# All steady projections, values and outputs in two turns on the array's 64-row halves, a job's first turn ahead of the sums

## The reference

```python
attn_in  = adaln(x, cond, ln1...)
x = attn(attn_in, attn_in, sa_wq, sa_wkv, sa_wo, sa_bo) + x      # 16 heads of 64
cross_in = adaln(x, cond, ln1...)
x = attn(cross_in, layernorm(context), ca_wq, ca_wkv, ca_wo, ca_bo) + x
x = gelu(adaln(x, cond, ln2...) @ ff_w1 + ff_b1) @ ff_w2 + ff_b2 + x
```

## Time and profile before

| | us |
|---|---|
| median of three runs | 1116.58 (1114.38 to 1116.66) |
| the profiled execution, its own time | 1118.88 |
| its span in the trace | 1117.1 |
| TensorE busy | 1097.2 (98%) |
| VectorE busy | 858.1 (77%) |
| GpSimd busy | 775.7 (69%) |
| ScalarE busy | 636.9 (57%) |

### The profile page before, as it was taken

How to read it: one execution, slowest core, us unless ns; L and a number is a source line. 1 busy time by engine, 2 the same in 40 slices (tenths; PEclk the granted TensorE clock), 3 DMA queues, 4 the chain that set the end, 5 groups by cost and what they waited for, 6 DMA issues and landing times.

```text
span 1117.1 us, 18312 instructions
## 1 busy us (share of the span) xinstructions
PE 1097.2 (98%) x6904; PEld 785.1 (70%) x6904; DVE 858.1 (77%) x1023; ACT 636.9 (57%) x895; POOL 775.7 (69%) x503
## 2 busy tenths in 40 slices
PE   8989999999999999999999999999999999989998
PEld 7657666776666776666766667766666776756997
DVE  5878887878787777878888777777877777788554
ACT  6465565665666555577665555555555545775521
POOL 2687887787788767789799766777777667755210
PEclk9899999999999999999999999999999999999999
DMA  6312121311231111211121112211121111300001
GB/s 175 86 46 57 32 53 39 89 30 30 53 77 38 39 36 23 72 39 39 29 63 38 39 39 59 51 23 36 38 72 39 37 31 30 114 1 1 20 19 38
DMA packets 59606, 52.31 MB, mean 47 GB/s; under 512 B 23040, under 2 KB 42496, under 8 KB 59264
## 3 DMA queue, kind: packets, MB, share of 16 engines
q1 hardware_dynamic: 57632, 49.57, 18.5%
q10 hardware_dynamic: 1888, 1.59, 0.5%
HBM read 15.22 MB, written 2.10 MB: 16 GB/s over the span
## 4 chain that ended last, share of the span: by engine, by line
PE 90%; DVE 5%; ACT 2%; issue 1%; DMA 1%; SPq 0%; POOL 0%; ACTq 0%; POOLq 0%; DVEq 0%
PE ps L872 18%; PE ps L713 12%; PE ps L715 11%; PE ps L714 11%; PE ps L813 6%; PE ps L860 6%; PE ps L848 5%; PE ps L819 5%; PE ps L815 5%; PE ps L817 5%; PE ps L963 4%; DVE lo L1083 1%; PE ps L729 1%; DMA x<-x_dram 1%; DVE w_lo L1117 1%
## 5 line engine op out<-in xcount | busy, mean ns | idle before, releaser
L548 ACT ACTIVATE probs<-ps 128x1024 f32<-128x1024 f32 x256 | 262.5, 1027 | 208.0 <-PE ps L819 183.6
L1065 DVE TENSOR_REDUCE neg_max<-ps 128x2 f32<-128x1024 f32 x256 | 301.6, 1226 | 76.7 <-PE ps L848 76.7
L420 POOL TENSOR_TENSOR acc<-acc,probs 128x1024 f32<-128x1024 f32 x128 | 306.2, 2392 | 18.6 <-POOL acc L415 0.4
L872 PE MATMUL ps<-probs,v 128*64 128x512 f32 x1024 | 230.7, 592 | 0.0
L415 POOL TENSOR_TENSOR acc<-probs 128x1024 f32<-128x1024 f32 x64 | 153.2, 2394 | 72.1 <-ACT probs L548 72.1
L872 PEld LDWEIGHTS ps<-probs,v 128*64 128x64 f32 x1024 | 73.9, 137 | 146.1 <-issue 146.1
L429 POOL TENSOR_TENSOR eo<-tmp 128x512 f32<-128x512 f32 x63 | 89.7, 1424 | 120.2 <-DVE tmp L1092 120.1
L1092 DVE TENSOR_TENSOR tmp<-ps,rope 128x1024 f32<-128x1024 f32 x126 | 148.2, 1211 | 4.5 <-PE ps L715 4.3
L813 PE MATMUL ps<-max_rows,pick 64*128 64x512 f32 x512 | 109.3, 419 | 2.6 <-DVE o_lo L1079 1.6
L713 PE MATMUL ps<-xn_hi,w_hi 128*128 128x512 f32 x256 | 107.8, 421 | 2.5 <-DVE o_lo L1079 1.3
L848 PE MATMUL ps<-hi 64*128 64x512 f32 x512 | 104.8, 400 | 5.4 <-DVE neg_max L1065 2.6
(11 more groups left out here) (116 smaller groups left out, 2250.0 us busy)
## 6 DMA issues: line engine op xcount, KB each, us to landing
lo<-eo SPq DMA_DIRECT2D x126, 256.0 KB, 3.2
w_raw<-pack_dram SPq DMA_DIRECT2D x16, 192.0 KB, 3.9
x<-x_dram SPq DMA_DIRECT2D x4, 512.0 KB, 7.5
w_raw<-pack_dram SPq DMA_DIRECT2D x8, 256.0 KB, 4.3
max_rows<-neg_max SPq DMA_DIRECT2D x128, 2.0 KB, 2.0
w_raw<-w_dram SPq DMA_DIRECT2D x2, 1024.0 KB, 5.8
out<-x SPq DMA_DIRECT2D x8, 256.0 KB, 2.2
ctx_in<-ctx_dram SPq DMA_DIRECT2D x4, 384.0 KB, 4.2
```

What stands on the lines that cost most here:

```text
L420: pool.tensor_tensor(acc[:, g % 2, :, :], acc[:, g % 2, :, :], probs[:, i, :, :], ALU.add).then_inc(added, 1)
L548: act.activation(probs[:, i, :, :], score_ps(i), ACT.Exp, scale=SCALE).then_inc(exped, 1)
L872: mm = pe.matmul(av_ps[DH * h:DH * h + DH, :], v[:, u % 2, kt, c:c + DH], probs[:, kt, h, :], start=(kt == 0), stop=(kt == TT - 1))
L1065: dve.tensor_reduce(neg_max[:, g % 2, :, i], peak_ps(i), AX.X, ALU.max, negate=True).then_inc(maxed, 1)
```

## The change

Jobs from 4 on, all values but the first and all outputs but the last are made in *two turns* of 64-row matmuls. In turn 0, one output takes its part of rows 0 to 63 and, beside it, another output its part of rows 64 to 127; in turn 1 they swap halves. Twelve matmuls of 128 rows so become 24 of 64 rows, side by side in twos. Turn 0 of a job stands ahead of `total`; it waits until the third peak is reduced, since the job now uses banks 4 and 5. Turn 1 stands where the projection stood. Values and outputs use banks 6, 7, 2, 3 (half of each) in most periods (`is_spread`). The context's 192 features are now 128 + 64 (the 64 are kept on both halves), so that a context key or value needs three quarters of the pairs. On DVE `low_qk(p + 2)` moves ahead of `normalise(p - 1)`, and on ScalarE `high_qk(p + 2)` ahead of `guess_inverse(p - 1)`. In the start, the rest of pair 1 goes from DVE to GpSimd, the first bias additions move to later periods (13, 15, 18, 21), and job 3 is placed between the first peaks. At the end, the last sums take two of the four probability tiles added by DVE, and the splits of the feed-forward weights are two DVE operations in place of eight.

```diff
-LOADS = (5, 7)
+LOADS = (5, 11)
...
         def job_ps(j, e):
-            return ps[:, (0, 2)[e] if j == 2 else 3 + e, :]
+            return ps[:, (0, 2)[e] if j == 2 else (3 if j < 4 else 4) + e, :]
...
-        bias_in.update({0: 0, 1: 1, 5: 2, 7: 3})
+        bias_in.update({13: 0, 15: 1, 18: 2, 21: 3})
...
+        def is_spread(p):
+            return 0 < p < PAIRS - 4 and p not in turned_in
+
+        def pair_of_banks(p, first, tt):
+            if is_spread(p):
+                return ps[:, ((6, 7), (2, 3))[tt % 2][tt // 2], 0:D]
+            return ps[:, first + tt // 2, tt % 2 * D:(tt % 2 + 1) * D]
```

TensorE's new helpers (`value_turn` is built like `out_turn`, with one part less in turn 1 for the context):

```diff
+            halves = (slice(0, 64), slice(64, 128))
+
+            def steps(turn, sparse):
+                return [(kt, part) for kt in range(KT if turn == 0 or not sparse else 1) for part in ((0, 0), (0, 1), (1, 0))]
+
+            def project_turn(j, turn):
...
+                if turn == 0:
+                    pe.wait_ge(maxed, 4 * (j - 3) + 3)
...
+                else:
+                    pe.wait_ge(half_projected, 2 * (j - 3))
+                a_ = (ctx_hi, ctx_lo) if on_ctx else (xn_hi, xn_lo)
+                todo = steps(turn, on_ctx)
+                for n, (kt, (wl, al)) in enumerate(todo):
+                    for e in range(2):
+                        half = halves[e ^ turn]
+                        c = slice(kt * 256 + e * 128, kt * 256 + (e + 1) * 128)
+                        mm = pe.matmul(job_ps(j, e), (w_hi, w_lo)[wl][half, k, c], a_[al][half, b, kt, :],
+                                       start=(turn == 0 and n == 0), stop=(turn == 1 and n == len(todo) - 1))
...
+            def out_turn(u, turn):
...
+                if turn == 0:
+                    pe.wait_ge(o_low, 2 * u + 2)
+                    pe.wait_ge(w_split, 4 * w + 4)
+                todo = steps(turn, False)
+                for t in range(2):
+                    if turn == 1:
+                        pe.wait_ge(half_out, 2 * u + 1 + t if is_spread(p) else 2 * u + 2)
+                    for n, (a, (ol, wl)) in enumerate(todo):
+                        for r in range(2):
+                            half = halves[r ^ turn]
+                            tt = 2 * r + t
+                            mm = pe.matmul(pair_of_banks(p, 6, tt), (o_hi, o_lo)[ol][half, a, tt * 128:(tt + 1) * 128],
+                                           (w_hi, w_lo)[wl][half, 3, a * D:(a + 1) * D],
```

`period(p)` on TensorE:

```diff
+                if is_job(p + 4):
+                    project_turn(p + 4, 0)
                 if is_pair(p - 1):
                     total(p - 1)
...
                     norm(turned_in[p], 0)
                     norm(turned_in[p], 1)
+
+                if p in v_in and not is_spread(p):
+                    value_turn(v_in[p], 0)
                 if is_job(p + 4):
-                    project(p + 4)
+                    project_turn(p + 4, 1)
+                if p in v_in and is_spread(p):
+                    value_turn(v_in[p], 0)
+                if p % 2 == 0 and is_quad(u - 1):
+                    out_turn(u - 1, 0)
                 if p in v_in:
-                    project_v(v_in[p], 0)
-                    project_v(v_in[p], 1)
+                    value_turn(v_in[p], 1)
                 if p % 2 == 0 and is_quad(u - 1):
-                    project_out(u - 1, 0)
-                    project_out(u - 1, 1)
+                    out_turn(u - 1, 1)
```

`period(p)` on VectorE (after its four peaks) and on ScalarE (after its four exponentials):

```diff
-                if p == 0:
-                    low_qk(1)
+                if is_pair(p + 2):
+                    low_qk(p + 2)
...
                 if is_pair(p - 1):
                     normalise(p - 1)
...
+                if p == PAIRS - 1:
+                    add_last_probs()
...
                 if p == PAIRS - 2:
-                    for c in range(4):
-                        split_ffw(0, c)
-                if is_pair(p + 2) and p not in stats_in:
-                    low_qk(p + 2)
+                    split_ffw(0)
                 if is_job(p + 4):
                     rotate(p + 4, 0)
                     rotate(p + 4, 1)
```

```diff
+                if is_pair(p + 2):
+                    high_qk(p + 2)
                 if is_pair(p - 1):
                     guess_inverse(p - 1)
                 if p in rows_in_period:
                     norm_rows(rows_in_period[p])
-                if is_pair(p + 2):
-                    high_qk(p + 2)
```

More of the change, by code:

```diff
@@ L325, in load_weights @@
                           .then_inc(w_loaded, 16)
[L326 to L329, removed]
+                        first, second = KT * 128, KT * 128 + 256
+                        for rows, kt, src, at in ((slice(0, CK), 0, slice(0, CK), first),
+                                                  (slice(CK, 128), 0, slice(0, 128 - CK), second),
+                                                  (slice(0, 64), 1, slice(128 - CK, CK), second),
+                                                  (slice(64, 128), 1, slice(128 - CK, CK), second)):
+                            sp.dma_start(raw[rows, 1:3, kt, a, :],
+                                         pack[src, at:at + 256].rearrange("p (m c) -> p m c", m=2))\
                               .then_inc(w_loaded, 16)
@@ L648, in _ @@
             high_qk(0)
+            high_qk(1)
             guess_rstd(2)
-            high_qk(1)
             norm_rows(2)
@@ L734, in project @@
                 u, k = j // 2, 1 - j % 2
[L735 to L741 removed]
+                b = quad(u)[1]
+                pe.wait_ge(w_split, place[k] + 1)
@@ L762, in project_v, with project_v_0 @@
+            def project_v_0():
+                pe.wait_ge(w_split, 3)
+                pe.wait_ge(rope_kept, 1)
+                for tt in range(TT):
+                    cut = slice(tt * 128, (tt + 1) * 128)
                     for kt in range(KT):
                         c = slice(kt * 256, (kt + 1) * 256)
-                        mm = parts(v_ps(u, r)[:, t * D:(t + 1) * D], a_hi[0:rows, b, kt, cut], a_lo[0:rows, b, kt, cut],
-                                   w_hi[0:rows, 2, c], w_lo[0:rows, 2, c], kt == 0, kt == KT - 1)
@@ L858, in total @@
                     pe.wait_ge(o_added, 2 * (QUADS - 1))
+                    pe.wait_ge(last_added, 1)
                 for h in range(2):
-                    mm = pe.matmul(sum_ps(g)[DH * h:DH * h + DH, :], ones[:, :], acc[:, g % 2, h, :], start=True, stop=True)
+                    out = sum_ps(g)[DH * h:DH * h + DH, :]
+                    mm = pe.matmul(out, ones[:, :], acc[:, g % 2, h, :], start=True, stop=g < PAIRS - 1)
+                    if g == PAIRS - 1:
+                        mm = pe.matmul(out, ones[:, :], tmp[:, 0, h, :], start=False, stop=True)
                 mm.then_inc(summed, 1)
@@ L1144, in period @@
                     rotate(p + 4, 1)
-                if is_pair(p + 2) and p in stats_in:
-                    low_qk(p + 2)
                 if p % 2 == 0 and is_quad(u - 1):
@@ L1150, in period @@
                 if p == PAIRS - 2:
-                    for c in range(4):
-                        split_ffw(1, c)
+                    split_ffw(1)
             norm_stats(0)
```

246 lines of the change are left out of this document (163 added, 83 removed).

## The result

The changed kernel took **1142.03 us** (median of 4 runs, 1141.07 to 1144.16), the kernel before 1115.48 (4 runs, 1114.35 to 1116.66): 1.0241 times as long, 95% interval 1.022 to 1.0261. That is 26.5 us more; 12 were forecast. The profiled execution took 1142.05 with a span of 1140.3.

A forecast was written before the change was run, and what follows sets the result against it. The prediction took TensorE, busy in the whole of each attention period, as the bound. Attention +23, start -7 and feed-forward's start -4 gave +12: span 1129, median 1128.5 us, range 1103 to 1143 (own range 1121 to 1136, chance 0.50).

The forecast's parts named there:

- TensorE's own price: Attention: one change of shape saved, -0.19 a spread period; context of 128 + 64 saves some 22 us; 256-column pairs cost 0.118.
- the slow pairs: Rival: some 1400 pairs of 256 columns cost more than 0.118; at 0.133 1149 us, at 0.233 +160; chance 0.10.
- The wait ahead of turn 0: Each attention period: turn 0 waits on TensorE for the third reduction, +0.45 us, covered by nothing.
- The chain of the outputs: Total to low_o: low_qk, held by GpSimd's addition, delays normalise; low_o ends at +12.95, outputs wait; even self periods 15.86.
- Two signs: Profile after: low_qk at 2.5 to 2.8 us in nearly all periods; a mid-attention clock below 1.00 would break the sum.
- first rival: Attention: outputs don't wait, low_o ends before turn 1 does; 23 us less, 1105 us; chance 0.25.
- second rival: Attention: the chain binds but GpSimd's additions don't block low_qk; low_o at +12.55, 10 us less, 1118; chance 0.15.
- even, self +0.82: Even self-attention periods take 15.86 us for 15.04; 13 of them, +10.7 us.
- The statistics term: Eight periods with a norm's statistics: low_o about 1.4 later, late rotation costs 0.5 in six, 1.2 in two, +5.4.
- at the feed-forward's start ... -4, bounds 0 and -6: End of the kernel: shorter splits and one addition less to wait for give -4 us.
- I take -7, bounds 0 and -10: Kernel start: low_qk(1) to GpSimd, an addition moved later and job 3 between peaks give -7 us.
- the median of the runs is 0.5 below the span: Last step: from a span of 1129 to a median of 1128.5 us.

The follow-up runs named there:

- experiment 5: Changed kernel with turn 0 behind the averages, the job whole ahead of the values, low_qk and high_qk in their old places: 1110.31 us, 0.9936 of the kernel before.
- experiment 6: Changed kernel with turn 0 behind the averages and the job whole ahead of the values; VectorE's and ScalarE's new order kept: 1144.78 us, 1.0254 of the kernel before.
- experiment 2: Changed kernel with low_qk and high_qk back in their old places, turn 0 still early: 1169.90 us, 1.0475 of the kernel before.
- experiment 4: Changed kernel with the context norm's rows moved behind the copy of the averages on ScalarE (periods 6, 10, 14, 18): 1138.92 us, 1.0198 of the kernel before.
- experiment 9: Changed kernel with context norm rows late, VectorE's old order in period 61, and turn 1 ahead of values in odd periods without spread banks: 1134.03 us, 1.0173.
- Experiment 7: Changed kernel with low_qk(63) and the statistics back behind normalise and low_o on VectorE in period 61 alone: 1141.44 us, 1.0224 of the kernel before.
- Experiment 11: Changed kernel with low_qk(1) back from GpSimd on VectorE, in period 0 ahead of low_qk(2): 1146.37 us, 1.0276 of the kernel before.
- experiment 3: Changed kernel with turn 0 behind the averages and low_qk and high_qk in their old places, nothing else: 1125.14 us, 1.0078 of the kernel before.
- experiment 10: Changed kernel with turn 0 between sums and averages, job whole ahead of values, low_qk and high_qk in old places, context norm's rows late: 1105.03 us, 0.9899.

## Why the prediction was right in sign and short in size

**TensorE's own price: right.** Pairs of 256 columns stand 0.114 apart among the outputs and 0.118 among the values, as forecast, and the 24 outputs take 444.05 - 441.20 = 2.85, first load included, so the lower bound was the right one and the slow pairs fell.

**The wait ahead of turn 0: right.** 433.32 is +5.00; counted from the end of the last peak's slot (432.98) it is 0.34, and 0.11 of open load comes on top (the next pair stands 0.34 on): 0.45, as forecast.

**The chain of the outputs: right, to 0.1 us.** `low_qk` ends at +9.4 (forecast 9.43), `low_o` at +12.83 (12.95), the steady periods are +0.17, +0.69, -0.48, +0.64 (+0.27, +0.82, -0.48, +0.84). In even self attention the missing tenth is that by which `low_o` ends earlier. Two signs came otherwise: `low_qk` takes 2.5 to 2.8 us in 31 of its 63 runs, not in nearly all, as it starts later in the even context periods; and the clock did fall in mid attention, in period 14. The first rival fell, and experiments 5 and 6 show the block itself: with `low_qk` behind `low_o` the outputs wait 1.1 us in all, ahead of `normalise` 18.0. The odd periods 29 to 35 show that it is GpSimd's addition that holds `low_qk`. But the block is only part of it: experiment 2 has no block, its `low_o` ends just as turn 1 does, and it is the slowest of all, as `low_qk` and the rotation then come late. With turn 0 early neither of the two orders that were tried on VectorE serves both. The second rival (the chain binds, no block, 1118) had left that out.

**Attention, +23 against +23.6: right, partly by luck.** The eight periods behind a norm's statistics (6, 10, 14, 18 and 28 to 34, even) were forecast at +7.7 together and are +12.1; all the others were forecast at +15.3 and are +11.5. In 6, 10, 14 and 18 the prediction's step "even, self +0.82" left out that ScalarE makes the norm's rows between the reciprocal and `o_hi`. Periods 6 and 14 are 16.80 and 19.41 long, the latter with a wait of 2.4 us for `low_o` and 3.4 us at half clock behind it. The statistics term (+5.4 of late rotation) was too large: of the 5.0 us for which peaks waited for a rotation, 2.7 lie in the start, 0.6 in the last periods, and 1.7 in periods 2 to 59. The errors cancel but for 0.6. Experiment 4 gave 4.4 us back in its four periods, and all three places of experiment 9 together 8.0 by the medians.

**The ends, -11 against -0.4: wrong, and this is the step that failed.** Three parts of it:

- The step "at the feed-forward's start ... -4, bounds 0 and -6" looked only at what stands behind the last periods. Its own part gave -2.1. But the new order on VectorE acts in periods 60 to 62 too, which the prediction put at nothing: they are +5.4, of which 4.5 in period 62 (19.21 for 14.73). Experiments 5 and 6, which differ in the order alone, are 40.54 and 47.46 long there, in period 60 15.31 and 18.01. VectorE in period 61:

```profile
1007.34 2.51 DVE L1240 TENSOR_TENSOR lo<-lo,hi 128x1024 fp32r<-128x1024 f32 x1 [0.54 <-ACT hi L610]
...
1013.89 0.69 DVE L1236 TENSOR_TENSOR o_lo<-ps,o_hi 128x512 fp32r<-128x512 f32 x1 [0.17 <-ACT o_hi L622]
1015.34 1.23 DVE L1222 TENSOR_REDUCE neg_max<-ps 128x2 f32<-128x1024 f32 x1 [0.76 <-PE ps L991]
```

  `low_qk(63)` and the statistics stand ahead of `normalise`, so `low_o` ends at 1014.58, and the peaks of pair 63, which want the bank of its sums, start 3.2 us late. Experiment 7 took 2.3 us of period 62 back.
- The step "I take -7, bounds 0 and -10" for the start gave -3.7: -3.3 ahead of period 0, +1.0 in period 0 and -1.4 in period 1. It was a choice between bounds without a chain behind it. Experiment 11 gives 1.8 us of it to `low_qk(1)` on GpSimd; what the other edits of the start are worth stays open. So does the term's true size, for it is one execution's: experiments 4 and 7 have the same code up to there and start period 2 at 72.92 and 78.27, with 3.4 and 20.4 us at half clock before it.
- The forecast's last step, "the median of the runs is 0.5 below the span", took a median and one execution for a fixed distance. Each execution's own time is 1.7 to 1.8 above its span in both kernels (1142.05 and 1140.3; 1118.88 and 1117.1). With 1117.1 + 12 + 1.8 the forecast would have been 1131.

The miss is 13.5 us, to rounding: 3.3 at the start, 0.6 in attention, 5.4 in periods 60 to 62, 1.9 behind them, and 2.2 for the last step.

**Where the change's own gain went.** In self attention 64-row turns save nothing over two periods (+0.15 each at best, experiments 5 and 8); experiment 3 has its odd periods 0.21 shorter, and pays for it in the even ones. The context in 128 + 64 rows makes most periods from 31 on 0.6 shorter. With VectorE's and ScalarE's order as before and the job whole ahead of the values, the kernel is 7.6 us faster than before (experiment 5); turn 0 between the sums and the averages and the norm's rows moved make that 10 (experiment 10). The two reorderings put back into experiment 5 cost 34 (experiment 6).

## What to carry to other kernels

Before an operation is moved ahead of a chain, work out what it waits for itself: `low_qk` waited for a landing, a copy and another engine's addition, and all three went into a chain with 1.4 us of slack. When a reordering goes into a loop, walk through the loop's odd iterations too (those with a norm, the last three); here they held about a third of the loss (8.0 of 26.5 us, experiment 9). And two edits that lengthen one chain should be tried apart and together: undoing one alone made it worse (1170) or no better (1145), undoing both made it 1110 (the last two with the job whole ahead of the values).

## What the runs showed of the hardware that was not expected

After single waits of 2.4 and 3.2 us in a stretch otherwise busy, TensorE went on at full clock, 2.4 GHz, and 1.1 to 1.3 us later its granted clock fell to half (1.2 GHz) for 3.4 us. The first of these, in the changed kernel's period 14:

```profile
280.54 0.38 PE L864 MATMUL ps<-w_hi,o_hi 64*128 64x256 f32 x2 [2.41 <-DVE o_lo L1236]
...
282.02 0.42 PE L864 MATMUL ps<-w_hi,o_lo 64*128 64x256 f32 x2
```

```profile
281.80:285.20 3.40, 3.40 (x34) 3.33 (x32) 1.80 (x3) 0.00 (x0) 2.37 (x2) 0.50 0.00 0
```

Pairs go from 0.12 to 0.21 apart, which costs about 1.5 us on top of the wait. In experiments 4 and 9 the same wait is 1.5 us long, and the clock of period 14 stays at 1.00 (the row shown of experiment 4). The length of one wait doesn't settle it, though. In the kernel before, waits of 0.63 and 1.27 us at the start of the feed-forward are followed by 3.4 us at half clock from 1018.8 on. And behind the same wait of 3.2 us period 62 has a mean clock of 0.91 in the changed kernel and of 0.83 in experiment 4.

A matmul that waits for TensorE's own results of just before it (turn 1 on turn 0) costs 0.34 us even though nothing else is in its way. With a turn of the values in between that is hidden (period 23 is 14.94 long in experiment 3 and 15.30 in experiment 5); with the averages in between too, but then each change between 64 and 128 rows costs 0.2 again.
